# First attention and first sparse layer in one block of instructions instead of two stages

## The reference

```
q, k, v = query @ Wq, key @ Wk, value @ Wv          # per head, width 16
out = softmax(q @ k.T * scale) @ v ;  x = x + out @ Wo

inter = xf @ c1_w.T @ c2_w.T                        # rank 16, 1792 wide
idx   = argmax of each block of 32 of inter         # one winner in each of 56 blocks
h     = relu(w1[idx] . xf)
out   = sum over the winners of h * w2t[idx]
```

## Time and profile before

| what | us |
|---|---|
| runs, in their order | 1524.52, 1518.81, 1521.06 |
| median | 1521.06 |
| span of the profiled execution | 1519.0 |
| attention, to the barrier before the sparse layer | 0 to 171.5 |
| sparse layer, to the last matmul of its last tile | 171.5 to 347.6 |
| all that follows | 347.6 to 1519.0 |
| PE busy over the span | 1394.3 (92%) |
| DVE, ACT, POOL busy | 1080.1, 762.1, 718.3 |

### The profile page before, as it was taken

One profiled execution on the slowest core, in us unless ns is written; L12 is line 12 of the kernel. 1 busy time (PEld: TensorE's weight loads), 2 busy tenths in 40 slices (PEclk: granted clock), 3 DMA queues, 4 the chain that ended last, 5 costly groups with the idle time before them and its releaser, 6 DMA issues. The chain is left out here.

```text
span 1519.0 us, 31488 instructions
## 1 busy us (share of the span) xinstructions
PE 1394.3 (92%) x11352; PEld 830.9 (55%) x11352; DVE 1080.1 (71%) x2125; ACT 762.1 (50%) x2476; POOL 718.3 (47%) x748
## 2 busy tenths in 40 slices
PE   5798599997999999887999999999999788889998
PEld 4676244445777777444655555555555335434444
DVE  7997665645666666667989888898877779966212
ACT  4777363222434432347666666666665457655111
POOL 4888551001433434845666666665665306734000
PEclk9999799999999999999999999999999898989999
DMA  7999572215999988766775655655545401546000
GB/s 189 186 174 181 124 171 42 35 35 122 174 195 184 170 142 136 127 144 147 154 150 112 113 115 111 140 109 115 105 79 79 123 3 32 127 84 112 17 12 28
DMA packets 524570, 174.63 MB, mean 115 GB/s; under 512 B 482576, under 2 KB 507600, under 8 KB 524416
## 3 DMA queue, kind: packets, MB, share of 16 engines
q1 hardware_dynamic: 524416, 172.62, 59.0%
HBM read 53.27 MB, written 2.10 MB: 36 GB/s over the span
## 5 line engine op out<-in xcount | busy, mean ns | idle before, releaser
L1946 POOL TENSOR_TENSOR a_q_ss<-a_q_ss,half 128x4 f32<-128x4 f32 x64 | 90.1, 1408 | 167.6 <-DVE a_q_ss L1855 84.0
L67 PE MATMUL bank<-a_wq_hi,xn_pair 128*128 128x512 f16 (+1 forms) x384 | 140.8, 367 | 10.9 <-DVE a_kn L1860 5.2
L1768 ACT ACTIVATE a_probs<-a_masked,a_negmax 128x128 f32<-128x128 f32 x256 | 99.6, 390 | 101.6 <-DVE a_negmax L1826 101.6
L1285 POOL TENSOR_TENSOR a_p_hl<-a_probs,a_p_hl 128x512 f16<-128x512 f32 x64 | 74.3, 1162 | 142.3 <-DVE a_p_hl L1209 142.3
L68 PE MATMUL bank<-a_wq_lo,xn_pair 128*128 128x512 f16 (+1 forms) x384 | 140.5, 366 | 0.0
L69 PE MATMUL bank<-a_wq_hi,xn_pair 128*128 128x512 f16 (+1 forms) x384 | 140.3, 365 | 0.0
L67 PE MATMUL bank<-a_wo_hi,a_o_hi 128*128 128x512 f16 x256 | 97.8, 382 | 4.4 <-DVE x_state L1842 3.5
L68 PE MATMUL bank<-a_wo_lo,a_o_hi 128*128 128x512 f16 x256 | 97.7, 382 | 0.0
L69 PE MATMUL bank<-a_wo_hi,a_o_lo 128*128 128x512 f16 x256 | 97.5, 381 | 0.0
L1961 POOL TENSOR_TENSOR a_normal<-a_probs,a_recip 128x512 f32<-128x512 f32 x64 | 90.2, 1410 | 5.0
L716 POOL TENSOR_TENSOR a_p_hl<-a_probs,a_p_hl 128x512 f16<-128x512 f32 x64 | 78.0, 1230 | 23.6 <-DVE a_p_hl L627 16.7
(11 more groups left out here) (467 smaller groups left out, 5022.4 us busy)
## 6 DMA issues: line engine op xcount, KB each, us to landing
a_no<-in_L_xattn_Wo SPq DMA_DIRECT2D x9, 1024.0 KB, 5.7
a_nq<-in_L_xattn_Wq SPq DMA_DIRECT2D x8, 1024.0 KB, 5.8
a_n_wq<-in_L_xattn_Wq SPq DMA_DIRECT2D x4, 768.0 KB, 5.7
a_n_wo<-in_L_xattn_Wo SPq DMA_DIRECT2D x4, 768.0 KB, 6.1
a_nk<-in_L_xattn_Wk SPq DMA_DIRECT2D x9, 256.0 KB, 3.0
a_nv<-in_L_xattn_Wv SPq DMA_DIRECT2D x9, 256.0 KB, 3.1
f_v_hat<-in_L_ffn_w SPq DMA_DIRECT2D x2, 1152.0 KB, 6.2
x_state<-in_x SPq DMA_DIRECT2D x8, 256.0 KB, 5.2
```

The lines of the kernel that those rows point to most:

```text
L67: pe.matmul(out, lh, rh, start=start, stop=False)
L1285: pool.tensor_tensor(p_hl[s % PN][:, 1, t, :], probs[unit(s, t) % PROBS][:, :, :].rearrange("p h n -> p (h n)"), p_hl[s % PN][:, 0, t, :], ...
L1768: m = act.activation(probs[s % 2][:, h, :], src, ACT.Exp, bias=negmax[s % 2][:, h:h + 1], accum_out=total[s % 2][:, h:h + 1])
L1946: pool.tensor_tensor(r[:, :], r[:, :], K.half[:, 0:n], ALU.pow).then_inc(root_done.sem, 1)
```

## The change

The two layers become one block. Each engine's program of a layer is now a Python generator that yields after each step; `in_turn` draws one step of the attention, then one of the sparse layer, which is `BESIDE = 73` steps behind. Step `s` of the sparse layer thus stands right after step `s + 73` of the attention on every engine. The barrier between them is gone; in its place, where the sparse layer takes over a buffer or a bank of the attention, it waits on the attention's own semaphores. `Front` is gone too: what it did is in the sparse layer's steps -25 to -9, beside units 48 to 64.

```diff
+BESIDE = 73
...
+def in_turn(a, b, shift, program_a, program_b):
+    for t in range(min(a.first, b.first + shift), max(a.end, b.end + shift)):
+        if a.first <= t < a.end:
+            next(program_a)
+        if b.first <= t - shift < b.end:
+            next(program_b)
...
 # first_attention
-    LOAD_SMALL, MEAN_FRONT, CLEAR_FRONT, HIGH_FRONT, LOW_FRONT, LOAD_FIRST = TOTAL - 14, TOTAL + 1, TOTAL + 2, TOTAL + 3, TOTAL + 10, TOTAL + 14
-    AHEAD = {B: TOTAL + 2, B + 1: TOTAL + 3, B + 2: TOTAL + 11, B + 3: TOTAL + 12}
+    LAST_OUT, LAST_ADD = TOTAL + 12, TOTAL + 13
+    out_at = lambda t, k: [b for b in at(t, OUT + k) if b < B - 1] + ([B - 1] if t == LAST_OUT else [])
+    add_at = lambda t: [b for b in at(t, ADD) if b < B - 1] + ([B - 1] if t == LAST_ADD else [])
...
+    def rows_used(engine):
+        engine.wait_ge(clo_done.sem, clo_done.count(last))
+        engine.wait_ge(xlo_done.sem, xlo_done.count(last))
...
+    def probs_turned(engine):
+        engine.wait_ge(plo_done.sem, plo_done.count(final))
+        for t in range(TOTAL - PB, TOTAL):
+            engine.wait_ge(p_in[t % PB], 16 * (t // PB + 1))
...
 # blocks_ffn
-    FIRST, LAG, RING, MASKS = -16, 2, 2, 4
-    NORM = {4: 2, 5: 3, 6: 4, 7: 5}
-    CX = {0: -9, 1: -8, 2: -7, 3: -6, 4: 4, 5: 5, 6: 6, 7: 7}
-    PICK = {(b, i): (4 * i - 5 if i else -7) + b if b < HALF else 4 * (i + 1) + b for b in range(B) for i in range(PARTS)}
-    SPLIT = {("w1", 0): -15, ("w2", 0): -5, ("w1", 1): -6, ("w2", 1): -4}
+    FIRST, LAG, RING, MASKS = -25, 4, 2, 4
+    LOAD_SMALL, LOAD_FIRST, LOAD_SECOND, MEANS, SMALL_HIGH, SMALL_LOW, LATER = -24, -23, -6, -19, -15, -9, 4
+    ROWS = {0: -16, 1: -14, 2: -12, 3: -10, 4: 5, 5: 6, 6: 7, 7: 8}
+    CX = {b: b - 9 if b < HALF else ROWS[b] + 1 for b in range(B)}
+    PICK = {(b, i): (4 * i - 5 if i else -8) + b if b < HALF else (4 * (i + 1) if i else 6) + b for b in range(B) for i in range(PARTS)}
+    SPLIT = {("w1", 0): -8, ("w2", 0): -3, ("w1", 1): -2, ("w2", 1): -1}
     SPLIT.update({(kind, q): 2 * q - 4 + i for q in range(2, PIECES) for i, kind in enumerate(("w1", "w2"))})
+    Y_BANKS, RING_BANKS = (2, 3, 4, 6), (5, 7, 0, 1)
...
+    mask_t = placed("probs0", [("mask_t", [P, NT, B * P], BF16)])["mask_t"]
+    on_scores = [("w1", 0), ("w2", 0), ("w1", 1)]
+    on_probs = [("w2", 1), ("w1", 2), ("w2", 2), ("w1", 3), ("w2", 3)]
...
 # sparse layer, SP
+        def turn_mask(part):
...
+            if part == parts[0]:
+                over.probs_turned(sp)
+            sp.wait_ge(pick_done.sem, pick_done.count(part))
...
+            if t == LOAD_SECOND:
+                over.queries_made(sp)
+                load(("w1", 1))
+                load(("w2", 1))
...
 # sparse layer, POOL
+        def constants():
+            over.keys_kept(pool)
+            pool.memset(cx_s[:, :], 0.0).then_inc(zeroed, 1)
+            over.weights_split(pool)
+            pool.memset(c2_s[:, :], 0.0).then_inc(zeroed, 1)
+            pool.memset(before[:, :], 1.0).then_inc(const_done, 1)
...
+        for t in steps:
+            if t == FIRST + 1:
+                constants()
...
 def stage_0_to_1(K, a, early):
     with ExitStack() as c:
-        front = Front(K, c, *(a[f"L0_ffn_{w}"] for w in ("c1_w", "c2_w", "w1", "w2t")))
-        first_attention(K, front, a["x"], a["ctx_t"], a["keep"], *(a[f"L0_xattn_{w}"] for w in ("Wq", "Wk", "Wv", "Wo")))
-        K.end_stage()
-        blocks_ffn(K, front, early)
-        K.in_use.append(front.first_in)
+        attention = first_attention(K, c, a["x"], a["ctx_t"], a["keep"], *(a[f"L0_xattn_{w}"] for w in ("Wq", "Wk", "Wv", "Wo")))
+        blocks = blocks_ffn(K, c, attention, *(a[f"L0_ffn_{w}"] for w in ("c1_w", "c2_w", "w1", "w2t")), early)
+        side_by_side(K.nc, attention, blocks, BESIDE)
```

More of the change, by code:

```diff
@@ L171, in low @@
                               self.K.xn_hi[:, :, b * P:(b + 1) * P], ALU.subtract).then_inc(self.ring.freed(b), 1)
[L174 to L200, removed]
@@ L208, in first_attention @@
+def first_attention(K, c, x_in, ctx_t, keep_in, wq, wk, wv, wo):
     nc = K.nc
@@ new lines, in first_attention, with high_ready, landed @@
+    heads_of = lambda t: [(2 * (t % 4) + j, ii) for ii in range(2) for j in range(2)]
+    copied_by = "VAVAVAVA"
+    by = lambda t, who: copied_by[t % UNITS] == who
+    phi_done = {who: Steps(sem(f"phi_{who}"), [u for u in units if by(u, who)]) for who in "VAP"}
+    def high_ready(engine, t):
+        done = phi_done[copied_by[t % UNITS]]
+        engine.wait_ge(done.sem, done.count(t))
+    weights_at = lambda t: [use for use, when in zip(pieces, WEIGHTS) if when == t]
+    def landed(engine, sems, b, n=1):
+        engine.wait_ge(sems[b % 2], 16 * n * (b // 2 + 1))
@@ new lines, in first_attention, with weights_split @@
+    stage = Stage(FIRST, END, sync, tensor, scalar, vector, gpsimd)
+    stage.place, stage.taken = place, taken
+    last, final = B - 1, TOTAL - 1
+    def weights_split(engine):
+        engine.wait_ge(wlo_done.sem, len(pieces))
+    def rows_used(engine):
+        engine.wait_ge(clo_done.sem, clo_done.count(last))
+        engine.wait_ge(xlo_done.sem, xlo_done.count(last))
+        for b in (last - 1, last):
+            landed(engine, xt_in, b)
+        engine.wait_ge(q_bank.filled(last), q_bank.n_filled(last))
@@ new lines, in blocks_ffn @@
+    xn, xn_hl = ([on_rows[f"{n}{i}"] for i in range(HALF)] for n in ("xn", "xn_hl"))
+    top = ring_of("top", MASKS, [P, SPAN * P // BLK], F32)
+    first_f, h = ring_of("first", 2, [P, HT], F32), ring_of("h", 2, [P, HT], F32)
+    h_hi, h_lo = ring_of("h_hi", LAG + 1, [P, HT], F16), ring_of("h_lo", LAG + 1, [P, HT], F16)
+    tiles, batches, ahead = list(range(TILES)), list(range(B)), list(NEXT)
+    live = lambda t: [t] if 0 <= t < TILES else []
+    at = lambda table, t: [use for use, when in table.items() if when == t]
@@ new lines, in width, with chosen, mask_landed, down_over @@
+    def width(part):
+        return min(SPAN, NT - SPAN * part[1]) * P
+    def chosen(part):
+        m, n = parts.index(part) % MASKS, width(part)
+        blocks = lambda t: t[:, 0:n].rearrange("p (n k) -> p n k", k=BLK)
+        return blocks(mask[m]), blocks(ring[("s", part)]), top[m][:, 0:n // BLK]
+    def mask_landed(engine, part):
+        engine.wait_ge(mask_in[parts.index(part) % MASKS], 16 * (parts.index(part) // MASKS + 1))
+    def down_over(engine, u):
+        if u % NT < NT - 1:
+            engine.wait_ge(down_done.sem, down_done.count(u))
+        else:
+            last = (u // NT, HALF - 1)
+            engine.wait_ge(y_bank.filled(last), y_bank.n_filled(last))
@@ L2505 @@
+    return Stage(FIRST, TILES + LAG + 1, sync, tensor, scalar, vector, gpsimd)
 class SecondWeights:
```

1620 lines of the change are left out of this document (814 added, 806 removed).

## The result

The change makes the kernel **slower**. Its median is 1531.91 us (four runs, 1528.01 to 1535.55) against 1520.35 us for the kernel before on the same chip (1518.81 to 1524.52): a ratio of 1.0076, 95% interval 1.0052 to 1.0100, or 11.6 us. Predicted were 1510.5 us and a range of 1502 to 1520. The profiled execution took 1531.26 us, its span is 1529.5; before, the span was 1519.0.

What follows compares the result with a forecast made beforehand. TensorE was taken as full from 196.1 us on, so only the seam before it could win: 196.36 - 183.5 (start of up(3)) - 2.3 (new wait) = 10.6 us saved, median 1521.06 to 1510.5, range 1502 to 1520.

Steps and rivals of the forecast that it cites:

- The mark to compare: Start of up(3) in the change: PE owes the same 151.2 us as at 196.36 before, when down(0) starts.
- PE waits for it: Before up(3): PE waits for the last heads' turned low part, at L + 17.9, then project_out(7) takes 2.6 us.
- L: End of the attention: when the last unit's probabilities land, 153.9 before, forecast at 163, with 159 to 168 as ends.
- the prediction's 17.9 us: From L to the landing of the last heads' turned low part, through masks, w1 and w2 pieces, ACT, POOL and SP.
- And from there on nothing waits: Sparse layer of the kernel before: once down(0) starts at 196.36, PE has no more waits.
- The new wait at the half: Steps 13 to 14: the mask of batch 7, columns 0 to 511, comes late; PE waits 2.3 us, between nothing and 3.
- Nothing taken: Attention's tail: DVE's row operations counted at nothing towards L, and likewise ACT's 3.7 us of small-weight splits.
- the megabyte near nothing: Attention's tail: loading the first weights costs the DMA engines between nothing and 5 us; taken near nothing.
- The tail gives it back: Rival, attention's tail: weights' 5 us or ACT's 3.7 us count, L 166.5 to 168, saving 5 to 7, about 1515; chance 0.31.
- The slower rival: Attention's tail: row chain blocks POOL and SP, L 175, up to 10 us slower, 1531; slower from 4.6 us a row; 0.07.
- Everything behind at nothing: Program behind the sparse layer's end (347.6 before): same program, one stage shift earlier, costed at nothing; 1171 us.
- The clock rival: Between L and up(3): scattered matmuls may leave PE's clock low, doubling work behind the mark; counted inside the cases, no own chance.

Runs made afterwards that it cites:

- e4: The change with attention output 6 added at step 74, compressions of batches 4 to 7 two steps behind their rows, first picks at steps 9 to 12: 1516.69 us, 0.9970.
- e2: The change, with DVE adding attention output 6 to x at attention step 74 instead of 76: 1524.17 us, ratio 1.0015 to the kernel before.
- e1: The change, with compressions of batches 4 to 7 three steps behind their rows instead of one: 1525.27 us, ratio 1.0036 to the kernel before.
- e3: The change, with first picks (masks) of batches 4 to 7 at steps 9 to 12 instead of 10 to 13: 1530.50 us, ratio 1.0056.
- f1: e4, with part of POOL's constants (2.2 of 3.85 us) moved from attention step 49 to 56: 1515.77 us, ratio 0.9963 to the kernel before.
- f3: e4, with ACT's high parts of the small weights at attention step 56 instead of 58: 1515.36 us, ratio 0.9965 to the kernel before.
- g1: e4 with the first megabyte loaded at attention step 59 instead of 50, and rows 2 and 3 made at 64 and 65, behind the last unit: 1514.42 us.
- g2: e4 with the first megabyte loaded at attention step 59 instead of 50, and high parts of rows 0 to 3 copied by ACT, not DVE: 1513.77 us.

## Why the prediction was wrong, point by point

- **The mark to compare** held. From the start of `up(3)` PE owes the same 151 us: e4 took 153.5, with two waits of 1.23 us inside.
- **"PE waits for it"** (the turned heads) is the step that failed ahead of the mark. The order of PE was read, but not what frees the y bank that `project_out(7)` writes: DVE's addition of output 6, which the change put behind three steps of the sparse layer. It measured 5.25 us of idle time and 1.8 of half clock; e2 moved the projection's end by 9.2 us, 3.3 of them an earlier mix. The chain ahead of it held: from the measured L, 168.9, the prediction's 17.9 us lead to heads that land at 186.8, and they landed near 188.2.
- **"And from there on nothing waits"** was said of the kernel before and carried over to the change. This is the step that failed behind the mark. The tables of rows and compressions for batches 4 to 7 moved too, to one step between a row and its compression; the chain of a row (DVE 0.9, POOL 1.2, SP's turn 4.7 to land) takes 7 us, and PE came to it after 2.6. No term of the sum had it. It cost 4.47 + 1.67 us idle and 7.2 in e1.
- **The new wait at the half** was right, at 2.97 us for 2.3, and too small as a term: with the half clock behind it the stretch lost 5.1 us in e3, some of it from the compression ahead.
- **L** was forecast at 163 and came near 168.9, beyond the later end of 168. Single terms were right: the constants took 3.9 us on POOL, the row turns 1.2 to 1.3 us each on SP. "Nothing taken" for DVE and for ACT, and the megabyte near nothing, were wrong: in 142.4 to 164.0 DVE was busy 21.29 of 21.60 us, PE waited 3.98 us for ACT behind its 3.7 us, and each turn behind the megabyte took 0.3 us more. The runs show no single term to charge the 5.9 us to; f1, f3, g1 and g2 each take one away and L stays. What part each has stays open.
- **The rivals.** "The tail gives it back" came nearest on L (166.5 to 168), and gave 1515; with the three waits out, e4 measures 1516.7. The slower rival's 1531 is within 1 us of the measured 1531.9, but that is luck, for its mechanism did not occur: POOL waited 0.36 us ahead of each row where it needed 4.6. The slowdown came from a mechanism that no rival had.
- **"Everything behind at nothing"**: 4.1 us less in the profile. Across kernels with identical code there the rest took from 1167.3 to 1172.9 us, so this is scatter and nothing of the change. The clock rival was put inside the cases: it took some 3.0 us behind the mark and 1.8 ahead of it, both behind waits that the sum did not have. The chances (0.07 for slower) were too sure: they rested on steps whose engines were checked one at a time.

## What to carry to other kernels

When two stages are interleaved by step, list for every PE instruction near the seam not only its data but the bank it writes, and find the instruction that frees it in the other stage's queue: a release that moved behind new work costs as much as late data. Give every chain through DVE, POOL and a turning DMA its measured length in steps, and move its consumer with it. If the engines of a stretch are each near full, do not price added work engine by engine; price its sum against all of them, or take it out of the stretch.
